# The token list of each expert found by one-hot masks and small matmuls, with the expert blocks of a scan and mixture-of-experts kernel begun at tile 3 and spread over more tiles

## What is computed

```
delta = softplus(xn @ Wd.T + dbias)                       # (B, L, 256)
Bs, Cs = xn @ WB.T, xn @ WC.T                             # (B, L, 256, 16) each
for t: h = exp(delta*A)*h + (exp(delta*A)-1)/A * Bs*xn ;  y_t = sum_n h*Cs
scores = xn @ Wr + br ; top 2 of 8, softmax over the two  # router
out = x + y + sum over the two experts w_e * (gelu(xn @ W1[e] + b1[e]) @ W2[e] + b2[e])
```

## Time and profile before

| | us |
|---|---|
| median of 3 runs | 1290.01 |
| profiled execution | 1290.72 |
| its span, first to last instruction | 1289.0 |
| TensorE busy | 1174.5 (91%) |
| VectorE busy | 977.8 (76%) |
| GpSimd busy | 835.1 (65%) |
| ScalarE busy | 803.8 (62%) |

### The profile page before, as it was taken

How to read it: one execution, slowest core, us unless ns; L and a number is a source line. 1 busy time by engine, 2 the same in 40 slices (tenths; PEclk the granted TensorE clock), 3 DMA queues, 4 the chain that set the end, 5 groups by cost and what they waited for, 6 DMA issues and landing times.

```text
span 1289.0 us, 22376 instructions
## 1 busy us (share of the span) xinstructions
PE 1174.5 (91%) x7674; PEld 730.4 (57%) x7674; DVE 977.8 (76%) x1362; ACT 803.8 (62%) x1341; POOL 835.1 (65%) x733
## 2 busy tenths in 40 slices
PE   1467887789899999999999999999999999999996
PEld 0342333455556666666666666666666666666652
DVE  6767998887777777777776866767777776776788
ACT  3553445577788775666567567576756657566631
POOL 2536788357878676665766676666675766667662
PEclk9998989999999999999999999999999999999998
DMA  9942234667768753445344354344444354334423
GB/s 295 301 126 103 80 107 141 229 209 233 260 210 270 235 139 111 119 102 141 104 111 131 93 138 131 90 121 134 105 124 122 100 136 119 107 114 105 103 62 138
DMA packets 87387, 186.96 MB, mean 145 GB/s; under 512 B 12784, under 2 KB 64880, under 8 KB 77168
## 3 DMA queue, kind: packets, MB, share of 16 engines
q1 hardware_dynamic: 59280, 152.80, 35.3%
q0 software_dynamic: 18000, 22.42, 10.6%
q10 hardware_dynamic: 10000, 10.38, 3.3%
HBM read 135.48 MB, written 57.96 MB: 150 GB/s over the span
## 4 chain that ended last, share of the span: by engine, by line
PE 72%; POOL 6%; DVE 6%; issue 5%; ACT 2%; DMA 1%; DVEq 0%; SPq 0%; POOLq 0%; ACTq 0%
PE bank L1165 39%; PE bank L1214 15%; PE bank L1227 15%; POOL xs L953 3%; DVE hb L1069 3%; POOL ax L938 2%; PE bank L1194 1%; PE bank L1239 1%; DVE bank L1047 1%; POOL whl L948 1%; DMA wst<-in_W 1%; DVE bank L1081 1%; PE bank L1246 1%; DVE ysum L1090 1%; DVE bank L1043 0%
## 5 line engine op out<-in xcount | busy, mean ns | idle before, releaser
L938 POOL TENSOR_TENSOR ax<-ax,x 128x512 f32<-128x512 f32 x214 | 272.1, 1279 | 287.2 <-ACT ax L843 285.2
L1165 PE MATMUL bank<-k_xT,k_WB 128*128 128x512 f16 x1536 | 379.5, 384 | 47.2 <-DVE hb L1069 34.4
L1165 PE MATMUL bank<-k_xT,k_WC 128*128 128x512 f16 x1536 | 377.0, 382 | 0.8 <-DVE ysum L1090 0.8
L1047 DVE TENSOR_TENSOR bank<-ax,bank 128x512 f32<-128x512 f32 x214 | 148.4, 693 | 222.9 <-PE bank L1165 197.9
L1165 PEld LDWEIGHTS bank<-k_xT,k_WB 128*128 128x128 f16 x1536 | 146.2, 99 | 200.8 <-DVE hb L1069 51.2
L1165 PEld LDWEIGHTS bank<-k_xT,k_WC 128*128 128x128 f16 x1536 | 151.4, 99 | 186.3 <-issue 7.2
L1069 DVE TENSOR_TENSOR_SCAN hb<-aexp,state,bank 128x512 f32<-128x512 f32 x192 | 244.4, 1273 | 0.0
L833 ACT ACTIVATE aexp<-k_dcur,k_A 128x512 f32<-128x512 f32 x256 | 180.8, 711 | 72.1 <-DVE hb L1069 66.8
L1214 PE MATMUL bank<-xbt,k_x 128*128 128x256 f16 x1872 | 218.7, 274 | 3.8 <-ACT k_x L881 3.8
L1214 PEld LDWEIGHTS bank<-xbt,k_x 128*128 128x128 f16 x1872 | 183.8, 98 | 42.9 <-ACT k_x L881 4.8
L1081 DVE SCALAR_TENSOR_TENSOR bank<-hb,k_rA,bank 128x512 f32<-128x512 f32 x240 | 179.9, 749 | 1.8
(11 more groups left out here) (144 smaller groups left out, 1321.6 us busy)
## 6 DMA issues: line engine op xcount, KB each, us to landing
k_x<-wsplit SPq DMA_DIRECT2D x78, 1024.0 KB, 4.8
wst<-in_W SPq DMA_DIRECT2D x32, 512.0 KB, 5.8
wsplit<-whl SPq DMA_DIRECT2D x32, 512.0 KB, 5.6
xs<-zero ACTq DMA_DIRECT2D x1, 10140.0 KB, 61.1
xb<-xs SPq DMA_DIRECT2D x39, 260.0 KB, 4.5
b<-in_b SPq DMA_DIRECT2D x39, 128.0 KB
k_x<-in_x SPq DMA_DIRECT2D x4, 1024.0 KB, 9.7
stB<-in_WBT SPq DMA_DIRECT2D x8, 512.0 KB, 10.0
```

The lines of the kernel that those rows point to most:

```text
L938: nc.gpsimd.tensor_tensor(ax[:, k % MR], ax[:, k % MR], x32[:], ALU.mult).then_inc(ax_done, 1)
L1047: v.tensor_tensor(bank, ax[:, RANK[g] % MR], bank, ALU.mult).then_inc(ux_done, 1)
L1165: ins = mm(bank[:], W[:, a, kc, n, hf * P:(hf + 1) * P], xT[:, c, b, kc, :], start=(k == 1), stop=(k == 3 * KC))
```

## The change

**The slot list is inverted on the chip.** Instead of scattering rows to slots, the kernel finds which token sits in each slot. A slot number is split into a high part (0 to 77, NS = NSLOT / 128) and a low part (0 to 127) by VectorE. For each of 2 choices and 32 token tiles it makes two fp16 masks with one tensor-scalar operation each: `hot_hi` is (column == high part) x token number, 128 x 78, and `hot_lo` is (column == low part), 128 x 128. TensorE multiplies them, 64 small matmuls that sum into bank 5, and the bank then holds the token number of each slot. Eight VectorE operations make of it `row` (where to read), `target` (where to add) and `second` (which choice). Token numbers run from -2048 to 2048 without 0, so that fp16 holds them exactly; row 2048 of `xrows` is a row of zeros for empty slots. The masks lie in the buffers stB, stC, xcur and soft, so VectorE waits until the prologue's other work on them is done.

**Rows.** All token rows with two extra columns go to memory (`xrows`, 4.2 MB) in the prologue, after the gate weights, which are now made ahead of the slots. `gather` on GpSimd fetches a block's 256 rows with two indirect DMAs, two blocks ahead. The zeroing of `xs`, the 64 scatters, `load_slots` and `slot_marks` are gone; `slot_data` has two operations instead of four.

**Pieces.** The first four weight pieces are split in the prologue (AHEAD = 4), and the piece buffers `wst` and `whl` are kept from there on. For their room aexp has 4 buffers instead of 5 and ax 3 instead of 4. The low half of the hidden layer of odd blocks has its own buffer beside the high one (`hs1`).

**Order.** Expert blocks start at tile 3, seven tiles each for the first eight, six for the others:

```
-META = 4
+META = 2
...
-E0 = 36
-EARLY, LONG, STEP = E, 6, 5
+E0 = 3
+EARLY, LONG, STEP = E, 7, 6
...
-        allowed = always + ([spare] if g < E0 - 2 or g >= E_END else [])
+        allowed = always + ([spare] if g >= E_END else [])
...
-PIECE_AT = {k: E0 - 18 + 4 * k if k < 4 else block_start((k - 4) // 4) + 3 + k % 4 for k in range(SPLITS)}
+AHEAD = 4
+PIECE_AT = {k: block_start((k - AHEAD) // 4) + 3 + k % 4 for k in range(AHEAD, SPLITS)}
...
-    AR, MR, HR = 5, 4, 3
+    AR, MR, HR = 4, 3, 3
...
-        act.wait_ge(zero_set, 1)
-        act.dma_start(io["xs"].rearrange("(p r) d -> p r d", p=P),
-                      zero[:].unsqueeze(1).broadcast_to([P, NSLOT // P, D + META])).then_inc(keep["zeros_out"], 16)
...
+        dve.wait_ge(gap_exp, 1)
+        ch.run(v.tensor_scalar(top[:], gate[:, 1, :], 1.0, None, ALU.add))
+        ch.run(v.reciprocal(gate[:, 0, :], top[:]))
+        ch.run(v.tensor_tensor(gate[:, 1, :], gate[:, 1, :], gate[:, 0, :], ALU.mult))
+        ch.run(v.tensor_copy(xall[:, :, D], gate[:, 0, :]))
+        ch.run(v.tensor_tensor(xall[:, :, D + 1], gate[:, 1, :], gate[:, 0, :], ALU.subtract))
+        dve.sem_inc(meta_set, 1)
...
+        ch.run(v.tensor_scalar(slot_hi[:], slotf[:], 1.0 / P, -(P / 2 - 0.5) / P, ALU.mult, ALU.add))
+        ch.run(v.tensor_scalar(slot_hi[:], slot_hi[:], ROUND, -ROUND, ALU.add, ALU.add))
+        ch.run(v.scalar_tensor_tensor(slot_lo[:], slot_hi[:], -float(P), slotf[:], ALU.mult, ALU.add))
+        dve.wait_ge(row_lo, 2 + NCH)
+        dve.wait_ge(delta_ready, 1)
+        dve.wait_ge(c_lo, 2 + NG)
+        for k in range(2):
+            for i in range(NT):
+                v.tensor_scalar(hot_hi[k][:, i], lane[:, 0:NS], slot_hi[:, k, i:i + 1], tid[:, i:i + 1],
+                                ALU.is_equal, ALU.mult)
+                ins = v.tensor_scalar(hot_lo[k][:, i], lane[:], slot_lo[:, k, i:i + 1], None, ALU.is_equal)
+                if i % (NT // 4) == NT // 4 - 1:
+                    ins.then_inc(lo_made, 1)
...
+        dve.wait_ge(table_made, 1)
+        table = banks[5][:, 0:2 * NS].rearrange("p (k s) -> p k s", k=2)
+        ch.run(v.tensor_copy(found[:], table))
...
+        ch.run(v.tensor_copy(keep["target"][:], row_f[:]))
...
+        for k in range(2):
+            for i in range(NT):
+                if i % (NT // 4) == 0:
+                    pe.wait_ge(lo_made, k * 4 + i // (NT // 4) + 1)
+                ins = mm(banks[5][:, k * NS:(k + 1) * NS], hot_lo[k][:, i], hot_hi[k][:, i],
+                         start=(i == 0), stop=(i == NT - 1))
...
+        def gather(b):
+            if b >= 2:
+                pool.wait_ge(turn_made, USE["turn", b - 2] + 1)
+                pool.wait_ge(w_set, b - 1)
+            for s in range(BS):
+                at = b * BS + s
+                nc.gpsimd.indirect_dma_start(
+                    out=xb32[:, b % 2, s], out_offset=None, in_=io["xrows"],
+                    in_offset=bass.IndirectOffsetOnAxis(keep["row"][:, at:at + 1], 0)).then_inc(xb_in[b % 2], 16)
```

More of the change, by code:

```diff
@@ L913, in _ @@
                 less_one(g + MR - 1)
-            for k in range(SPLITS):
+            for k in range(AHEAD, SPLITS):
                 if PIECE_AT[k] == g:
-                    high_piece(k)
+                    high_piece(nc, act, keep, k)
     @block.gpsimd
```

448 lines of the change are left out of this document (222 added, 226 removed).

## The result

The changed kernel takes **1385.0 us** (median of 4 runs, 1383.2 to 1386.9) beside 1290.4 us of the kernel before on the same chip: ratio 1.073, 95% interval 1.070 to 1.076. The prediction was 1341 (1300 to 1368): slower was right, the size was not, and the time lies above the range.

What follows compares the result with a forecast made beforehand. TensorE, full in the late stage, bounds the kernel. First scan 138.5, first part 11 + 27 + 218 + 10, late blocks 861.5 + 32, end 31.8 + 9.7: span 1339.5, forecast 1341 us (1300 to 1368).

Steps and rivals of the forecast that it cites:

- What bounds the kernel, and what is moved: Whole kernel: TensorE is full in the late stage; work can only move into idle elsewhere, at most some 40 us.
- A: 31 late blocks: one tile more without expert work, with a 0.75 us scan wait; 27.79 us each, 861.5 in all.
- B: Shorter aexp and ax rings: nine late blocks with an early z part stall, 32 us; ordinary blocks lose nothing in the sum.
- C: Start to early blocks: three tiles 11 us, block 0 27, blocks 1 to 7 218, stalls 10 (0 to 25).
- D: End of the kernel: ten tiles 31.8 us, tail 8.7, plus 1 for the later last accumulate (0 to 6).
- E: Prologue: first scan at 138.5 us instead of 109.1, with 22.4 us for the masks at 0.35 a pair.
- what I said of the Trainium skill: Prologue masks: its two elements a cycle would give about 15 us; the trace speaks against it for per-partition scalars.
- Only the rings don't bite: Late blocks with z parts: ax comes in time; 1309 us, or 1304 with fewer early stalls; chance 0.16.
- The rings bite in every block: Ordinary blocks have no slack either and lose 1 us in each of 30 more; 1371 us, chance 0.13.
- The masks are dearer: Prologue: each mask slowed by GpSimd or with 0.2 us overhead of its own; 15 us more, 1356, chance 0.06.
- Faster: Two B banks suffice, so uncovered tiles cost nothing and late blocks take 27.04 us; 1260 us in all, chance 0.08.

Runs made afterwards that it cites:

- e13: The changed kernel with four down parts, longer rings from tile 38, broadcast masks, z parts, low halves, gathers and rows' accumulates moved, copy to acc held back; 1286.3 us.
- e5: The changed kernel with four down parts instead of three and, from tile 60 on, the rings of before; 1307.4 us, ratio 1.013.
- e3: The changed kernel with the rings of before (5 buffers of exponentials, 4 of ax) from tile 60 on; 1333.0 us, ratio 1.033.
- e2: The changed kernel with the down product cut into four parts instead of three; 1378.7 us, ratio 1.068.
- e9: The changed kernel with GpSimd's low half of a weight piece made one tile earlier; 1382.5 us, ratio 1.070.
- e1: The changed kernel with the z parts (softplus of the next chunk) moved to the last tile of a block; 1342.4 us, ratio 1.040.
- e16: The changed kernel with the row 0 to 127 that every mask compares kept in 16 bits instead of 32; 1381.4 us, ratio 1.072.
- e7: The changed kernel with two extra masks before 20 of the token-number masks, run once: 0.17 us comparison alone, 0.17 with a constant, 0.23 with the token number.
- e4: The kernel before with only the rings shortened, 4 buffers of exponentials and 3 of ax instead of 5 and 4; 1398.1 us, ratio 1.083.

## Why the prediction was wrong

**What bounds the kernel, and what is moved.** Right. TensorE is full in the late stage, and only its idle could be won; e13 wins it.

**A, late blocks.** The size was nearly right: 27.4 and 27.8 us against 27.79, with the wait once per block, as in the earlier trace rows. Its price was read from the bracket, 0.75; from start to start it costs 0.92 (e5), 5 us in 31 blocks. That is most of the 6.4 us by which the late stage exceeds 861.5 even with long rings (e3, 867.9). The cause was half of it: e2 and e5 show a second one, a late ax, hidden behind the first.

**B, shorter rings: the step that failed most.** The sum took 32 us for them. The nine blocks, the engine and the wait were right: 32.5 us against 32. But B took that wait for the whole cost of the shorter rings, and e3 measures 47.4, above even its upper bound of 9 x 5. Two terms were put at nothing. TensorE's clock falls behind the wait in seven of the nine blocks, 1.7 us each, 12 us. And the two blocks with a z part in their third tile, "where I find no wait", lose 3.0. For ordinary blocks "no loss in the sum" was true of the total only, because both waits fall together. With A, this is the +21.8 us of the late stage.

**C, the first part.** 10 us of stalls were taken, 19.6 came. 4.2 are block 1's wait for the store of a piece (e9); that the ax ring of 3 puts GpSimd, and so the low half that the store waits for, a tile later against ScalarE was argued, not tried. 4.9 came back by the z parts' place (e1). With all mends the stage takes 249.8 us (e13), 5 less than forecast, and its granted clock is 1.00 instead of 0.98. The remaining stalls were not taken apart.

**D, the end.** 3.7 us short in all. With longer rings the last tiles take 32.7 (e3, e13), so 1.5 us belonged to the short rings as well. The tail is 8.9 in e3 but 10.3 in e13, and what sets it was not followed.

**E, the prologue.** 138.5 forecast, 146.0 measured, at the upper bound. The masks without interference cost 0.43 us a pair instead of 0.35, 5 us in 64 pairs: I had read one slope and one offset from two kinds of instructions, eight operations of 256 elements with two per-partition scalars and a pair of 2 elements that were of another operation. With 0.13 us fixed, 0.06 for the second scalar and 0.5 ns per element, the first of those rows gives 0.32, which is what it shows (0.334). The measured values refute what I said of the Trainium skill (VectorE: DVE Perf Modes, "Mode 2x_2P"): its rule of two elements a cycle holds here, per-partition scalars included, at 0.5 ns per element; and with 16-bit elements its four a cycle ("Mode 4x_2P") agree with e16. What my estimate of 15 us had too small is the fixed part: 0.07 us of it, where e7 shows 0.13, two thirds of a mask of 128, and 0.06 for the second scalar. GpSimd's low halves took 4.0 us from the masks (forecast 4.5), but also 2.7 from two operations before them, which was not in the sum:

```profile
98.16 0.61 DVE L640 TENSOR_TENSOR tmp<-oh,cs 128x256 f32<-128x256 f32 x1 [0.16 <-DVE k_x L637]
...
99.26 1.97 DVE L640 TENSOR_TENSOR tmp<-oh,cs 128x256 f32<-128x256 f32 x1
...
101.72 1.55 DVE L643 TENSOR_SCALAR slot_hi<-slotf 128x64 f32<-128x64 f32 x1
103.31 0.20 DVE L644 TENSOR_SCALAR slot_hi<-slot_hi 128x64 f32<-128x64 f32 x1
```

The wait for ScalarE's exponential was 3.7 us (forecast 2.7). Against that, the removed zeroing gave 3.8 (3) and reading the table back took 2.1 (3.4): its casts take 0.20 us each. The 1.77 of the old cast ended at 100.14, with a GpSimd operation that ran from 97.40 to 100.09, so it was such a wait too and no price of a cast.

**The rivals.** "Only the rings don't bite" is refuted by e3 and e4. "The rings bite in every block" did not happen in the new order, but e4 shows it of most blocks of the old. (Its 1371 us lay outside the range that was said to reach to it.) "The masks are dearer" came true by a third of its price. "Faster" is out: two banks do not suffice for an uncovered tile. Its late blocks of 27.04 us are nearly reached (27.2 in e5 and e13), but by leaving no tile uncovered.

## What to carry to other kernels

When a buffer is taken from a ring, cost the stall and what follows it: behind most of the stalls here TensorE's granted clock fell, and that cost over a third as much once more. A wait that goes away and comes back as long in the next place has two causes; take both away before calling either harmless. An idle in brackets can be less than a wait costs; read it from start to start. And a fixed cost and a cost per element are only told apart by rows of the same operation with the same operands at two sizes.
